# Tail exponentials stacked in rows for two of four head groups, and the heads' scores issued ahead of the previous group's values

## The chip, the cores and the metric

The kernel runs on one core of one Trainium2 chip. The metric is the device time of one execution in microseconds (us), the median over runs. The profiler's times come from one further execution of the same program.

## The reference: what is computed

The input x has 4 sequences of 2048 tokens with 512 channels; the context has 4 sequences of 154 tokens. All is float32. Cut to what matters:

```python
# gated cross attention: 16 heads of 32 channels, 154 keys per head
Q = (layernorm(x) @ Wq.T); K = ctx @ Wk.T; V = ctx @ Wv.T
attn = softmax(Q K^T / sqrt(32)) V                   # per head
x = x + tanh(g_xattn) * (attn @ Wo.T)
# gated feed-forward with a shift by one token
n = layernorm(x); prev = n shifted by one token
xr = mu_r*n + (1-mu_r)*prev; xk = mu_k*n + (1-mu_k)*prev
x = x + tanh(g_ffn) * sigmoid(xr @ W_r.T) * (relu(xk @ W_k.T)**2 @ W_v.T)
```

## The kernel before

The tokens are cut into 16 blocks of 512 (`N`). Block `i` does its attention while TensorE also does the feed-forward of block `i - 1`; block 0 has the projections of the context in that place. Blocks 1 to 14 are one hardware loop, blocks 0 and 15 are written out. `ffn` is true for every block but the first, `pre` for every block but the last. "Later blocks" are blocks 1 to 15.

Every product is made in parts: a number is split into a high part and the rest, and three products are summed (high by high, high by low, low by high; `PRODUCTS`). The order on each engine is written out by hand, and semaphores carry the dependences; each engine runs its own list in order.

The 16 heads are four groups (`g`) of four. For one group the work is:

- `head_scores` (L1512 to L1525, TensorE): scores of the first 128 keys of each of the four heads, one bank `s_bank[j]` for each, as matmuls on a quarter of the array's rows. It waits until all low parts (`p_lo`) of the group before have been made.
- `tail_scores` (L1527 to L1532): the other 26 keys of all four heads in one bank, with 32 rows for each head. It waits until the low part of unit 0 of this group is made, because it writes the same bank.
- `exps` (L791 to L798, ScalarE): for each of the five banks (`n` = 0 to 4, the tails are 4), one exponential into the high part in `pq` (16 bit) and one, in place in the bank, in full precision.
- `p_low` (L1097 to L1099, VectorE): the full exponential minus the high part, into the low part in `pq`.
- `values` (L1534 to L1553, TensorE): the values product into `o_bank` (12 matmuls for the heads, 12 for the tails), and the sums of the exponentials into `d_bank` (8 and 8). They use a quarter of the array's columns each, so that four run beside each other.
- `attend` (L1101 to L1116, VectorE): two transposes, a reciprocal and a product, which make the group's normalised result `attn32`. `attn_high` (ScalarE) and `attn_low` (GpSimd) split it.

Between these, TensorE has products of 12 matmuls of 512 columns of the feed-forward (`ffn_r`, `ffn_v`). In a later block the order on TensorE from group 1 on is: `values(0)`, `head_scores(1)`, `ffn_r(1)`, `tail_scores(1)`, `ffn_v(0)`, `values(1)`, `head_scores(2)`, `ffn_v(1)`, `tail_scores(2)`, `ffn_r(2)`, `values(2)`, `head_scores(3)`, `ffn_r(3)`, `tail_scores(3)`, `ffn_v(2)`, `values(3)`.

During the same groups the next block's input is prepared. VectorE takes its statistics (`moments1`, L1037 to L1042), ScalarE normalises (`norm1_turn`, L742), VectorE turns it (`turn`, L1077: the first two tiles in group 2 before `p_low(2, 2)`, the others after `gated`), and SyncE stores the two halves to memory and loads them again transposed (`store_turned` L346, `load_turned` L353). ScalarE and GpSimd split what was loaded (`xT_high_half` L690, `xT_low_half` L544), VectorE has one part of that (`xT_low_part` L1082) and then does `attend(3)`. After `values(3)` TensorE makes the next block's queries in halves (`query_half`, L1502) and, inside the last of them, the first row maxima (`maxima(i + 1, 0)`, L1478). `maxima(i + 1, 0)` waits for `q_high(i + 1, 0)`, which on ScalarE stands behind `attn_high(i, 3)`.

`gated` (L1126) is VectorE's last step on a feed-forward product. `load_values` (L373, L374) brings the next block's values to SBUF.

Of the kernel before, what the change touches and what calls it, by code (L numbers as in the profile page):

```python
# [17 lines left out]
def flamingo_block(nc, x, ctx_columns, g_xattn, g_ffn, Wq, Wk, Wv, Wo, W_r, W_k, W_v, mu_r, mu_k, out):  # L18
# [34 lines left out]
    with ExitStack() as ctx:  # L53
# [14 lines left out]
        def parts(name):  # L68
# [3 lines left out]
            parts(n) for n in ("WqT", "WoT", "WrT", "WkT2", "WvT2"))  # L72
        xnT_loaded, xnT = parts("xnT")
# [13 lines left out]
        v_tail = sb("v_tail", [P, 2, G, 4, TAIL], F16)  # L87
        ones_main = sb("ones_main", [P, DH], F16)
        ones_tail = sb("ones_tail", [P, 4, DH], F16)
        xa = sb("xa", [P, TT, D], F32)  # L90
        x1 = sb("x1", [P, TT, D], F32)
        pq = sb("pq", [P, 5, 2, N], F16)
        place = sb("place", [P, 8, N], F32)
        mm = sb("mm", [P, TT, P], F32)
# [19 lines left out]
        recip = sb("recip", [P, N // 32], F32)  # L114

# [62 lines left out]
        p_hi, p_full, p_lo = sem("p_hi"), sem("p_full"), sem("p_lo")  # L178
# [49 lines left out]
        K_LOADS, V_LOADS, FIRST_TAILS = 7, 5, 5  # L228
# [62 lines left out]
        def _(sp):  # L291
# [76 lines left out]
            def load_values(i):  # L368
                later(sp, av_done, i * G)
                b = i // PER_BATCH  # L370
                for j in range(4):
                    rows = slice(DH * j, DH * j + DH)
                    sp.dma_start(v_tail[rows, :, :, j, :], vt_scratch[b].rearrange("r s (g j d) -> r s g j d", g=G, j=4)[:, :, :, j, :]).then_inc(v_loaded, 16)  # L373
                sp.dma_start(v_main[:, :, :], v_scratch[b]).then_inc(v_loaded, 16)  # L374
# [94 lines left out]
        def _(pool):  # L469
            done = [0]  # L470

            def link(ins):
# [15 lines left out]

            link(nc.gpsimd.memset(ones_main[:, :], 1.0))
# [4 lines left out]
                                         base=DH - 1, pattern=[[DH, 4], [0, DH]], channel_multiplier=-1))  # L494
            link(nc.gpsimd.memset(tail_rows[:, :], 1.0))
# [9 lines left out]
            link(nc.gpsimd.memset(mm[:, :, :], 0.0))  # L505
# [182 lines left out]
        def _(act):  # L688
# [21 lines left out]
            def kv_high(u):  # L710
                item, kind, n = KV[u]
                act.wait_ge(kv_done, u + 1)
                if item == 1 and kind == "k" and n >= 2:
                    act.wait_ge(later_stored[n - 2], 48)
                elif (item, kind, n) == (1, "v", 0):
                    act.wait_ge(v_stored, 32)
                    act.wait_ge(v_loaded, 16 * V_LOADS)
# [73 lines left out]
            def exps(i, g, n):  # L791
# [72 lines left out]
            def step(i, ffn, pre):  # L864
# [9 lines left out]
                exps(i, 0, 0)  # L874
                exps(i, 0, 1)
# [3 lines left out]
                exps(i, 0, 2)  # L879
                exps(i, 0, 3)  # L880
                if not ffn:
                    kv_high(FIRST_LATER)
                exps(i, 0, 4)
# [6 lines left out]
                for g in range(1, G):  # L890
                    exps(i, g, 0)
                    exps(i, g, 1)
                    attn_high(i, g - 1)
# [4 lines left out]
                    exps(i, g, 2)  # L898
                    exps(i, g, 3)
                    if not ffn and g < 3:  # L900
                        kv_high(FIRST_LATER + 2 * g)
                    exps(i, g, 4)
# [101 lines left out]
        def _(dve):  # L1004
# [80 lines left out]
            def reduce_max(i, r, heads=range(4)):  # L1085

                (g, t), pairs = ROUNDS[r][0], len(ROUNDS[r])
                for j in heads:
                    if r == j == 0:
                        later(dve, mT_done, i)  # L1090
                    dve.wait_ge(max_done, i * MAX_UNITS + 4 * r + j + 1)
                    scores = s_bank[j][:, 0:S * pairs].rearrange("p (n s) -> p n s", n=pairs)
                    column = TAIL * j + g
                    maxima = mm[:, t:t + pairs, column] if ROUNDS[r][-1][1] > t else mm[:, t, column:column + pairs]
                    nc.vector.reduce_max(maxima, scores, AX.X).then_inc(reduced, 1)  # L1095

            def p_low(i, g, n):  # L1097
                dve.wait_ge(p_full, i * SCORE_UNITS + 5 * g + n + 1)
                nc.vector.tensor_tensor(pq[:, n, LO, :], score_bank[5 * g + n][:, :], pq[:, n, HI, :], ALU.subtract).then_inc(p_lo, 1)  # L1099
# [130 lines left out]
            def step(i, ffn, pre):  # L1230
# [16 lines left out]
                p_low(i, 0, 0)  # L1247
                if ffn:
                    xr_low(i - 1, 3)
                p_low(i, 0, 1)  # L1250
                p_low(i, 0, 2)
                p_low(i, 0, 3)
                if not ffn:
                    kv_low_part(FIRST_LATER)
                p_low(i, 0, 4)
# [7 lines left out]
                for g in range(1, G):  # L1263
                    attend(i, g - 1)
                    p_low(i, g, 0)
                    p_low(i, g, 1)
# [7 lines left out]
                    p_low(i, g, 2)  # L1274
                    p_low(i, g, 3)
                    if not ffn and g < 3:
                        kv_low_part(FIRST_LATER + 2 * g)
                    p_low(i, g, 4)
# [130 lines left out]
        def _(pe):  # L1409
# [97 lines left out]
            def maxima_transposed(i):  # L1507
                pe.wait_ge(reduced, (i + 1) * MAX_UNITS)
                later(pe, x2_ready, i * TT - 1)
                transposed(mT_bank, [mm[:, t, :] for t in range(TT)]).then_inc(mT_done, 1)  # L1510
# [23 lines left out]
            def values(i, g, by_pe):  # L1534
                pe.wait_ge(p_lo, i * SCORE_UNITS + 5 * g + 5)
                later(pe, attn32_ready, i * G + g)
                if g == 0:
                    pe.wait_ge(v_loaded, 16 * V_LOADS * (i + 1))
# [3 lines left out]
                for n in range(2):  # L1542
                    for k, (s, q) in enumerate(PRODUCTS):
                        for j in range(4):
                            v = v_main[:, s, DH * (4 * g + j):DH * (4 * g + j + 1)] if n == 0 else v_tail[:, s, g, j, :]
                            nc.tensor.matmul(o_bank[rows(j), :], v, pq[:, 4 if n else j, q, :],  # L1546
                                             start=(n, k) == (0, 0), stop=(n, k) == (1, 2))
                for n in range(2):
                    for q in (HI, LO):
                        for j in range(4):  # L1550
                            one = ones_main[:, :] if n == 0 else ones_tail[:, j, :]
                            ins = nc.tensor.matmul(d_bank[rows(j), :], one, pq[:, 4 if n else j, q, :],  # L1552
                                                   start=(n, q) == (0, HI), stop=(n, q) == (1, LO))  # L1553
# [57 lines left out]
            def ffn_r(i, t):  # L1611
# [3 lines left out]
                else:  # L1615
                    pe.wait_ge(u_ready, i * TT + t)
                product(R_BANK[t][:, :], lambda s, c: buf2[:, s, c, cols(t)], lambda m, c: WrT[:, m, c, :], C,
                        (lambda c: pe.wait_ge(xr_lo, i * C + c + 1)) if t == 0 else None).then_inc(r_done, 1)
# [37 lines left out]
            def step(i, ffn, pre):  # L1656
# [26 lines left out]
                tail_scores(i, 1)  # L1683
                if ffn:
                    ffn_v(i - 1, 0)
                else:
                    keys_or_values(FIRST_LATER + 3)
                values(i, 1, not ffn)

                head_scores(i, 2)  # L1690
                if ffn:
                    ffn_v(i - 1, 1)
                else:
                    keys_or_values(FIRST_LATER + 4)
                tail_scores(i, 2)
                if ffn:
                    ffn_r(i - 1, 2)
                else:
                    keys_or_values(FIRST_LATER + 5)
                values(i, 2, not ffn)  # L1700

                head_scores(i, 3)
                if ffn:
                    ffn_r(i - 1, 3)
                else:
                    keys_or_values(KV_UNITS - 1)
                if not ffn:
                    xT(1, 0)
                tail_scores(i, 3)
                if ffn:  # L1710
                    ffn_v(i - 1, 2)
                else:
# [129 lines left out]
```

## Time and profile before

| | |
|---|---|
| runs | 1353.62 us median of 3 (1349.99 to 1354.55) |
| the profiled execution's own time | 1352.5 us |
| its span | 1350.8 us |
| matmuls on TensorE | 9776, busy 98% of the span |
| VectorE, ScalarE, GpSimd busy | 77%, 58%, 49% |
| mean granted TensorE clock | 0.997 |

The span is the stretch from the first to the last instruction of the profile; the execution's own time has 1.7 us more around it. Busy shares are means over the whole program. In the rows further below, a line of the timeline is a run of equal instructions merged into one: its start and length in us, the engine, the line of the kernel, the operation, what it writes and reads, how many there are, and in brackets how long the engine stood idle before it and which instruction ended that. Matmuls overlap, so that the start of the next line says more than the length of one. PEld is TensorE's weight load, SPq is SyncE's DMA queue.

### The profile page before, as it was taken

How to read it: one execution, taken by the hardware profiler on the slowest of the kernel's cores; microseconds unless marked ns; L12 is line 12 of the kernel's file. 1: busy time of each engine (PE TensorE's matmuls, PEld its weight loads, DVE VectorE, ACT ScalarE, POOL GpSimd, SP SyncE). 2: the span in 40 equal slices, each digit the busy share in tenths (PEclk: the TensorE clock that was granted, in tenths of full speed). 3: DMA queues.
4: the chain of work that ended last, by engine and by line, in shares of the span. 5: the costliest groups of instructions: out<-in, count | busy, mean ns of one | idle time of the engine just before them, and what ended most of it. 6: DMA issues, size and time to landing. Idle time of an engine off the chain costs nothing.

```text
span 1350.8 us, 28900 instructions
## 1 busy us (share of the span) xinstructions
PE 1324.2 (98%) x9776; PEld 992.8 (73%) x9776; DVE 1046.6 (77%) x1983; ACT 778.0 (58%) x1457; POOL 659.6 (49%) x843
## 2 busy tenths in 40 slices
PE   6999999999999999999999999999999999999998
PEld 5667687777768677776877768777776877768777
DVE  6878778787886878778787887878788687877763
ACT  7655737466474655737466473745737465573633
POOL 7524445454444545445454445545445554444434
PEclk9998999999999999999999999999999999999999
DMA  9521312424123242312424222242413324231011
GB/s 311 155 59 48 91 51 78 116 55 128 44 84 77 62 132 54 99 45 77 112 54 132 59 77 66 62 132 54 122 33 85 93 54 139 54 92 48 32 48 40
DMA packets 160732, 113.27 MB, mean 84 GB/s; under 512 B 107456, under 2 KB 122304, under 8 KB 160704
## 3 DMA queue, kind: packets, MB, share of 16 engines
q1 hardware_dynamic: 160704, 112.91, 29.3%
q8 instruction: 16, 0.26, 0.1%
q14 instruction: 12, 0.10, 0.0%
HBM read 72.43 MB, written 35.39 MB: 80 GB/s over the span
## 4 chain that ended last, share of the span: by engine, by line
PE 88%; DVE 8%; ACT 3%; issue 1%; DMA 0%; DVEq 0%; ACTq 0%
PE g_bank L1415 41%; PE g_bank L1606 10%; PE o_bank L1546 7%; PE g_bank L1502 6%; PE s_bank L1520 4%; PE d_bank L1552 4%; PE s_bank L1530 3%; PE s_bank L1415 3%; PE s_bank L1478 3%; DVE buf L1006 2%; DVE o_bank L1194 2%; PE o_bank L1421 1%; DVE d_bank L1194 1%; PE s_bank L1524 1%; PE d_bank L1421 1%
## 5 line engine op out<-in xcount | busy, mean ns | idle before, releaser
L1099 DVE TENSOR_TENSOR pq<-s_bank,pq 128x512 f16<-128x512 f32 x320 | 220.0, 688 | 73.4 <-ACT s_bank L798 72.1
L1095 DVE TENSOR_REDUCE mm<-s_bank 128x3 f32<-128x462 f32 (+1 forms) x384 | 198.8, 578 | 74.6 <-PE s_bank L1478 74.6
L797 ACT ACTIVATE pq<-s_bank 128x512 f16<-128x512 f32 x320 | 194.3, 607 | 101.2 <-PE s_bank L1524 101.2
L798 ACT ACTIVATE s_bank<-s_bank 128x512 f32<-128x512 f32 x320 | 197.0, 616 | 0.0
L1606 PE MATMUL g_bank<-buf,WkT 128*128 128x512 f32 x720 | 189.7, 409 | 3.4 <-DVE buf L1006 3.3
L1415 PE MATMUL g_bank<-WrT,buf 128*128 128x512 f32 x744 | 183.7, 396 | 0.0
L1415 PE MATMUL g_bank<-WoT,buf 128*128 128x512 f32 (+1 forms) x768 | 175.4, 374 | 0.0
L1415 PE MATMUL g_bank<-WvT,buf 128*128 128x512 f32 x708 | 174.3, 395 | 0.0
L1415 PEld LDWEIGHTS g_bank<-WrT,buf 128*128 128x128 f32 x744 | 137.2, 188 | 39.3 <-issue 10.8
L1606 PEld LDWEIGHTS g_bank<-buf,WkT 128*128 128x128 f32 x720 | 131.4, 191 | 43.9 <-DVE buf L1006 9.6
L1415 PEld LDWEIGHTS g_bank<-WvT,buf 128*128 128x128 f32 x708 | 130.7, 188 | 32.4 <-issue 5.4
L568 POOL TENSOR_TENSOR buf<-place,buf 128x512 fp32r<-128x512 f32 x64 | 82.7, 1293 | 141.6 <-ACT buf L690 141.6
L1415 PEld LDWEIGHTS g_bank<-WoT,buf 128*128 128x128 f32 x768 | 131.2, 188 | 26.0
L690 ACT ACTIVATE buf<-place 128x512 fp32r<-128x512 f32 (+1 forms) x132 | 82.7, 626 | 72.6 <-DVE place L1116 46.4
L556 POOL TENSOR_TENSOR buf<-xa,buf 128x512 fp32r<-128x512 f32 x64 | 82.5, 1289 | 84.5 <-ACT xa L776 46.6
L564 POOL TENSOR_TENSOR buf<-place,buf 128x512 fp32r<-128x512 f32 x60 | 78.1, 1301 | 79.9 <-ACT buf L690 79.9
L1415 PE MATMUL g_bank<-xnT,WqT 128*128 128x512 f32 x420 | 110.9, 401 | 0.0
L576 POOL TENSOR_TENSOR x<-place,x 128x512 f32<-128x512 f32 x45 | 57.9, 1287 | 99.3 <-DVE place L1126 99.3
L757 ACT ACTIVATE xa<-x,nb,rstd 128x512 f32<-128x512 f32 x48 | 39.2, 816 | 112.0 <-POOL nb L525 111.8
L1502 PE MATMUL g_bank<-xnT,WqT 128*128 128x256 f32 x672 | 87.9, 287 | 0.0
L1502 PEld LDWEIGHTS g_bank<-xnT,WqT 128*128 128x128 f32 x672 | 82.1, 191 | 7.1 <-issue 5.9
L1415 PEld LDWEIGHTS g_bank<-xnT,WqT 128*128 128x128 f32 x420 | 74.3, 188 | 14.8 <-issue 0.4
(186 smaller groups left out, 2304.6 us busy)
## 6 DMA issues: line engine op xcount, KB each, us to landing
xa<-in_x SPq DMA_DIRECT2D x64, 256.0 KB, 4.2
x<-in_x SPq DMA_DIRECT2D x64, 256.0 KB, 2.8
xt_scratch<-xa SPq DMA_DIRECT2D x28, 512.0 KB, 3.1
xnT_loaded<-xt_scratch SPq DMA_DIRECT2D x112, 128.0 KB, 3.2
out<-x SPq DMA_DIRECT2D x48, 256.0 KB, 2.3
place<-x SPq DMA_DIRECT2D x16, 256.0 KB, 2.4
out<-place SPq DMA_DIRECT2D x16, 256.0 KB, 2.0
k_all<-k_scratch SPq DMA_DIRECT2D x15, 256.0 KB, 3.3
```

The source lines that it names most:

```text
L556: nc.gpsimd.tensor_tensor(buf4[:, LO, g, :], q32[g], buf4[:, HI, g, :].bitcast(F32), ALU.subtract).then_inc(q_lo, 1)
L564: nc.gpsimd.tensor_tensor(buf1[:, LO, c, :], k2[c % 2], buf1[:, HI, c, :].bitcast(F32), ALU.subtract).then_inc(k2_lo, 1)
L568: nc.gpsimd.tensor_tensor(buf3[:, LO, g, :], attn32, buf3[:, HI, g, :].bitcast(F32), ALU.subtract).then_inc(attn_lo, 1)
L690: nc.scalar.activation(dst, src, ACT.Copy).then_inc(done, 1)
L797: nc.scalar.activation(pq[:, n, HI, :], bank[:, :], ACT.Exp, scale=SCALE).then_inc(p_hi, 1)
L798: nc.scalar.activation(bank[:, :], bank[:, :], ACT.Exp, scale=SCALE).then_inc(p_full, 1)
L1095: nc.vector.reduce_max(maxima, scores, AX.X).then_inc(reduced, 1)
L1099: nc.vector.tensor_tensor(pq[:, n, LO, :], score_bank[5 * g + n][:, :], pq[:, n, HI, :], ALU.subtract).then_inc(p_lo, 1)
L1415: ins = nc.tensor.matmul(dst, stationary(s, c), moving(m, c), start=(c, n) == (0, 0), stop=(c, n) == (chunks - 1, len(PRODUCTS) - 1))
L1502: ins = nc.tensor.matmul(tokens_of(Q_BANK[g][:, :], h), WqT[:, s, c, cols(g)], tokens_of(xnT[:, m, c, :], h), start=(n, c) == (0, 0), stop ...
L1546: nc.tensor.matmul(o_bank[rows(j), :], v, pq[:, 4 if n else j, q, :], start=(n, k) == (0, 0), stop=(n, k) == (1, 2))
L1606: ins = nc.tensor.matmul(K_BANK[c][:, :], WkT2[:, s, e, cols(c)], buf3[:, m, e, :], start=(e, n) == (0, 0), stop=(e, n) == (C - 1, len(PRO ...
```

## The change

In later blocks, groups 1 and 3 (`STACKED`) hold the tails' exponentials otherwise. The high part of the first two heads goes to rows 0 to 63 of one 512-column tile and that of the last two to rows 64 to 127 of a second; the low parts go to the other half of the rows. So the high and the low part of one head lie in one column of the array's input. This takes two high exponentials on 64 rows each in place of one on 128, a wait on their end before the full exponential, and two subtractions on 64 rows in place of one. The values product for the tails then has 8 matmuls in place of 12, the sums 4 in place of 8. The values of the tails are loaded to a second set of rows (four more DMAs in `load_values`), and a second pattern of ones (`ones_both`) is made once at the start on GpSimd.

In all groups of later blocks the order on TensorE changes: `head_scores(g + 1)` stands ahead of `values(g)`, and `tail_scores` stands inside the product that follows, ahead of its third chunk of four. So that this can be, the exponentials of even groups go to buffers of their own, `p_even` (in the room of `xnT`'s high part) and `p_even_tail`, and `exps` waits for the values of the group before the last one. On VectorE `attend(g - 1)` moves behind `p_low(g, 0)`, on ScalarE `attn_high(g - 1)` behind `exps(g, 4)`. The tile `mm` of the maxima shrinks from 512 to 140 columns with the blocks' columns laid between each other.

```diff
             def xT_high_half(i, h, part):
                 act.wait_ge(xT_loaded[h], (i - 1) * 64)
+                act.wait_ge(av_done, i * G - 1)
...
-                later(act, av_done, i * G + g)
-                nc.scalar.activation(pq[:, n, HI, :], bank[:, :], ACT.Exp, scale=SCALE).then_inc(p_hi, 1)
+                later(act, av_done, i * G + g - 1 if ffn else i * G + g)
+                place = p_place(ffn, g, n)
+                if n < 4 or not stacked(ffn, g):
+                    nc.scalar.activation(place[:, HI, :], bank[:, :], ACT.Exp, scale=SCALE).then_inc(p_hi, 1)
+                else:
+                    for tile, rows in enumerate(tail_halves):
+                        nc.scalar.activation(place[rows, tile, :], bank[rows, :], ACT.Exp, scale=SCALE).then_inc(p_tail_hi, 1)
+                    act.wait_ge(p_tail_hi, 2 * ((i - 1) * len(STACKED) + STACKED.index(g) + 1))
                 nc.scalar.activation(bank[:, :], bank[:, :], ACT.Exp, scale=SCALE).then_inc(p_full, 1)
...
+                    for tile, rows in enumerate(tail_halves):
+                        ins = nc.vector.tensor_tensor(place[tail_halves[1 - tile], tile, :], bank[rows, :], place[rows, tile, :], ALU.subtract)
+                    ins.then_inc(p_lo, 1)
...
                 for g in range(1, G):
-                    attend(i, g - 1)
-                    p_low(i, g, 0)
-                    p_low(i, g, 1)
+                    if not ffn:
+                        attend(i, g - 1)
+                    p_low(i, g, 0, ffn)
+                    if ffn:
+                        attend(i, g - 1)
+                    p_low(i, g, 1, ffn)
...
+                if stacked(not by_pe, g):
+                    for s in (HI, LO):
+                        for j in range(4):
+                            nc.tensor.matmul(o_bank[rows(j), :], v_tail[:, s, g, j, :], places[4][:, j // 2, :], start=False, stop=s == LO)
...
+                if stacked(not by_pe, g):
+                    for j in range(4):
+                        ins = nc.tensor.matmul(d_bank[rows(j), :], ones_both[:, j % 2, :], places[4][:, j // 2, :], start=False, stop=True)
...
-                values(i, 0, not ffn)
-
-                head_scores(i, 1)
-                if ffn:
-                    ffn_r(i - 1, 1)
+                if ffn:
+                    head_scores(i, 1)
+                values(i, 0, not ffn)
+                if ffn:
+                    ffn_r(i - 1, 1, at(2, lambda: tail_scores(i, 1)))
+                    ffn_v(i - 1, 0)
```

## Rows read from the trace of the kernel before

**Rows 1.** The page's first part, busy time of each engine over the span.

```profile
PE 1324.2 (98%) x9776; PEld 992.8 (73%) x9776; DVE 1046.6 (77%) x1983; ACT 778.0 (58%) x1457; POOL 659.6 (49%) x843
```

**Rows 2.** Timeline of TensorE in one middle block, values(0) to the next block's queries.

```profile
619.01 0.83 PE L1546 MATMUL o_bank<-pq,v_main 128*32 128x512 f16 x12
619.67 0.82 PE L1546 MATMUL o_bank<-pq,v_tail 128*32 128x512 f16 x12
620.31 0.61 PE L1552 MATMUL d_bank<-pq,ones_main 128*32 128x512 f16 x8
620.75 0.61 PE L1552 MATMUL d_bank<-pq,ones_tail 128*32 128x512 f16 x8
621.28 0.74 PE L1520 MATMUL s_bank<-buf,k_all 32*128 32x512 f32 x8
622.41 3.02 PE L1415 MATMUL g_bank<-WrT,buf 128*128 128x512 f32 x12
625.26 0.86 PE L1530 MATMUL s_bank<-buf,k_tail 128*128 128x512 f32 x3
626.19 2.90 PE L1415 MATMUL g_bank<-WvT,buf 128*128 128x512 f32 x12
629.02 0.83 PE L1546 MATMUL o_bank<-pq,v_main 128*32 128x512 f16 x12
651.33 5.53 PE L1502 MATMUL g_bank<-xnT,WqT 128*128 128x256 f32 x44
656.81 0.57 PE L1478 MATMUL s_bank<-k_all,buf 32*128 32x154 f32 x12
```

**Rows 3.** Timeline of ScalarE in the same block: groups 0 and 1.

```profile
620.94 0.63 ACT L690 ACTIVATE buf<-place 128x512 fp32r<-128x512 f32 x1 [1.22 <-POOL place L560]
622.59 0.60 ACT L797 ACTIVATE pq<-s_bank 128x512 f16<-128x512 f32 x1 [1.02 <-PE s_bank L1524]
623.09 0.59 ACT L798 ACTIVATE s_bank<-s_bank 128x512 f32<-128x512 f32 x1
```

**Rows 4.** Timeline of VectorE in the same block: groups 1 and 2.

```profile
628.23 0.69 DVE L1099 TENSOR_TENSOR pq<-s_bank,pq 128x512 f16<-128x512 f32 x1 [0.31 <-ACT s_bank L798]
629.21 0.69 DVE L1126 SCALAR_TENSOR_TENSOR place<-place,g_bank 128x512 f32<-128x512 f32 x1 [0.28 <-PE g_bank L1415]
631.67 0.68 DVE L1110 STREAM_TRANSPOSE place<-d_bank 128x512 f32<-128x512 f32 x1
634.03 1.38 DVE L1099 TENSOR_TENSOR pq<-s_bank,pq 128x512 f16<-128x512 f32 x2
635.32 1.30 DVE L1077 STREAM_TRANSPOSE xa<-place 128x512 f32<-128x512 f32 x2
```

**Rows 5.** Timeline of SyncE's queue in the same block and just ahead of it.

```profile
606.57 0.37 SPq L378 DMA_DIRECT2D out<-place  x1
636.65 0.33 SPq L346 DMA_DIRECT2D xt_scratch<-xa  x1
645.94 2.61 SPq L353 DMA_DIRECT2D xnT_loaded<-xt_scratch  x4
658.71 2.86 SPq L373 DMA_DIRECT2D v_tail<-vt_scratch  x4
```

**Rows 6.** Timeline of ScalarE and VectorE in the same block, behind the second load.

```profile
651.86 1.15 ACT L690 ACTIVATE xnT<-xnT_loaded 128x512 fp32r<-128x512 f32 x2 [2.10 <-DMA xnT_loaded<-xt_scratch]
652.52 0.69 DVE L1082 TENSOR_TENSOR xnT<-xnT_loaded,xnT 128x512 fp32r<-128x512 f32 x1 [2.60 <-ACT xnT L690]
655.64 0.63 ACT L690 ACTIVATE buf<-place 128x512 fp32r<-128x512 f32 x1 [2.62 <-DVE place L1116]
656.17 0.58 ACT L690 ACTIVATE buf<-g_bank 128x512 fp32r<-128x512 f32 x1
```

**Rows 7.** Timeline, the same place six blocks later.

```profile
1134.37 5.53 PE L1502 MATMUL g_bank<-xnT,WqT 128*128 128x256 f32 x44
1137.85 0.63 ACT L690 ACTIVATE buf<-place 128x512 fp32r<-128x512 f32 x1 [2.66 <-DVE place L1116]
1139.83 0.57 PE L1478 MATMUL s_bank<-k_all,buf 32*128 32x154 f32 x12
```

More of the change, by code:

```diff
@@ L72, in flamingo_block @@
             parts(n) for n in ("WqT", "WoT", "WrT", "WkT2", "WvT2"))
+        with nc.sbuf_tensor("p_even", [P, 4, 2, N], F16) as p_even:
+            pass
         xnT_loaded, xnT = parts("xnT")
@@ L114, in flamingo_block, with p_place, stacked @@
         recip = sb("recip", [P, N // 32], F32)
+        def p_place(ffn, g, n):
+            if ffn and g % 2 == 0:
+                return p_even[:, n, :, :] if n < 4 else p_even_tail[:, :, :]
+            return pq[:, n, :, :]
+        tail_halves = (slice(0, 2 * DH), slice(2 * DH, P))
+        STACKED, stacked_groups = (1, 3), slice(1, G, 2)
+        def stacked(ffn, g):
+            return ffn and g in STACKED
         k2 = (place[:, 0, :], place[:, 1, :])
@@ L372, in load_values @@
                     rows = slice(DH * j, DH * j + DH)
-                    sp.dma_start(v_tail[rows, :, :, j, :], vt_scratch[b].rearrange("r s (g j d) -> r s g j d", g=G, j=4)[:, :, :, j, :]).then_inc(v_loaded, 16)
+                    other = slice(DH * ((j + 2) % 4), DH * ((j + 2) % 4) + DH)
+                    tails = vt_scratch[b].rearrange("r s (g j d) -> r s g j d", g=G, j=4)
+                    sp.dma_start(v_tail[rows, :, :, j, :], tails[:, :, :, j, :]).then_inc(v_loaded, 16)
+                    sp.dma_start(v_tail[other, HI, stacked_groups, j, :], tails[:, HI, stacked_groups, j, :]).then_inc(v_loaded, 16)
                 sp.dma_start(v_main[:, :, :], v_scratch[b]).then_inc(v_loaded, 16)
@@ L873, in step @@
                     xr_high(i - 1, 2)
-                exps(i, 0, 0)
-                exps(i, 0, 1)
+                exps(i, 0, 0, ffn)
+                exps(i, 0, 1, ffn)
                 if ffn:
@@ L890, in step @@
                 for g in range(1, G):
-                    exps(i, g, 0)
-                    exps(i, g, 1)
-                    attn_high(i, g - 1)
+                    exps(i, g, 0, ffn)
+                    exps(i, g, 1, ffn)
+                    if not ffn:
+                        attn_high(i, g - 1)
                     if not ffn and g == 3:
@@ L897, in step @@
                         xT_high(i + 1, 0)
-                    exps(i, g, 2)
-                    exps(i, g, 3)
+                    exps(i, g, 2, ffn)
+                    exps(i, g, 3, ffn)
                     if not ffn and g < 3:
                         kv_high(FIRST_LATER + 2 * g)
-                    exps(i, g, 4)
+                    exps(i, g, 4, ffn)
+                    if ffn:
+                        attn_high(i, g - 1)
                     if ffn and pre:
@@ L1092, in reduce_max, with p_low @@
                     scores = s_bank[j][:, 0:S * pairs].rearrange("p (n s) -> p n s", n=pairs)
[L1093 to L1094 removed]
+                    column, stride = TAIL * j + 4 * t + g, 4 if ROUNDS[r][-1][1] > t else 1
+                    maxima = mm[:, column:column + stride * (pairs - 1) + 1:stride]
                     nc.vector.reduce_max(maxima, scores, AX.X).then_inc(reduced, 1)
[L1097 removed]
+            def p_low(i, g, n, ffn):
                 dve.wait_ge(p_full, i * SCORE_UNITS + 5 * g + n + 1)
[L1099 removed]
+                place = p_place(ffn, g, n)
+                bank = score_bank[5 * g + n]
+                if n < 4 or not stacked(ffn, g):
+                    nc.vector.tensor_tensor(place[:, LO, :], bank[:, :], place[:, HI, :], ALU.subtract).then_inc(p_lo, 1)
+                else:
+                    for tile, rows in enumerate(tail_halves):
+                        ins = nc.vector.tensor_tensor(place[tail_halves[1 - tile], tile, :], bank[rows, :], place[rows, tile, :], ALU.subtract)
+                    ins.then_inc(p_lo, 1)
             def attend(i, g):
@@ L1509, in maxima_transposed @@
                 later(pe, x2_ready, i * TT - 1)
-                transposed(mT_bank, [mm[:, t, :] for t in range(TT)]).then_inc(mT_done, 1)
+                transposed(mT_bank, [mm[:, 4 * t:4 * t + P] for t in range(TT)]).then_inc(mT_done, 1)
             def head_scores(i, g):
@@ L1541, in values @@
                     pe.wait_ge(xT_lo, TT + 1)
-                for n in range(2):
+                places = [p_place(not by_pe, g, n) for n in range(5)]
+                for k, (s, q) in enumerate(PRODUCTS):
+                    for j in range(4):
+                        nc.tensor.matmul(o_bank[rows(j), :], v_main[:, s, DH * (4 * g + j):DH * (4 * g + j + 1)], places[j][:, q, :],
+                                         start=k == 0, stop=False)
+                if stacked(not by_pe, g):
+                    for s in (HI, LO):
+                        for j in range(4):
+                            nc.tensor.matmul(o_bank[rows(j), :], v_tail[:, s, g, j, :], places[4][:, j // 2, :], start=False, stop=s == LO)
+                else:
                     for k, (s, q) in enumerate(PRODUCTS):
                         for j in range(4):
[L1545 to L1548, printed above, removed]
+                            nc.tensor.matmul(o_bank[rows(j), :], v_tail[:, s, g, j, :], places[4][:, q, :], start=False, stop=k == 2)
+                for q in (HI, LO):
+                    for j in range(4):
+                        nc.tensor.matmul(d_bank[rows(j), :], ones_main[:, :], places[j][:, q, :], start=q == HI, stop=False)
+                if stacked(not by_pe, g):
+                    for j in range(4):
+                        ins = nc.tensor.matmul(d_bank[rows(j), :], ones_both[:, j % 2, :], places[4][:, j // 2, :], start=False, stop=True)
+                else:
                     for q in (HI, LO):
                         for j in range(4):
-                            one = ones_main[:, :] if n == 0 else ones_tail[:, j, :]
-                            ins = nc.tensor.matmul(d_bank[rows(j), :], one, pq[:, 4 if n else j, q, :],
-                                                   start=(n, q) == (0, HI), stop=(n, q) == (1, LO))
+                            ins = nc.tensor.matmul(d_bank[rows(j), :], ones_tail[:, j, :], places[4][:, q, :], start=False, stop=q == LO)
                 ins.then_inc(av_done, 1)
```

83 lines of the change are left out of this document (47 added, 36 removed).

## Prediction, made before the changed kernel ran

> **What bounds the kernel now.** First the busy line [rows 1]: TensorE is busy for 98% of the span, no other engine for more than 77%. So work taken off TensorE can be worth its time, but only where nothing else stands just behind it. The timelines tell that, and I read them for one middle block, TensorE first. With T for the start of values(1) at 629.02, its queries start at 651.33 (call this point Q, T + 22.31) and the maxima at 656.81 (call it M, Q + 5.48) [rows 2]. Then I looked, on the other engines, for what ends just before TensorE needs it. There are two such places. One is the last low part of each group: the subtraction of group 1 starts at 628.23 and lasts 0.69, so it ends at 628.92, 0.1 ahead of T [rows 2, 4]. The other is M. The chain to it starts with the first pair of turns on VectorE (635.32), goes over store and load (SyncE issues the store at 636.65 and the second load at 645.94), the split on ScalarE at 651.86, VectorE's part at 652.52, then attend(3), attn_high(3) at 655.64, and q_high at 656.17 + 0.58 = 656.75 [rows 4 to 6]. TensorE starts the maxima at 656.81, 0.06 later. So in this block M has no slack at all, although TensorE shows no idle time there.
>
> **What TensorE loses.** The tails' part of a values product is 12 matmuls in 620.31 - 619.67 = 0.64, three rounds of four, so 0.213 a round; the sums over the heads are 8 in 620.75 - 620.31 = 0.44, or 0.22 a round [rows 2]. A stacked group saves one round of each, 0.433. Two groups in 15 blocks: 0.87 a block, 13.0 us in all. This is the whole gross gain.
>
> **Order on TensorE.** Nothing else is removed. values(0) takes 621.28 - 619.01 = 2.27, head_scores 622.41 - 621.28 = 1.13, a product 2.83 to 2.85, tail_scores 626.19 - 625.26 = 0.93 [rows 2], before and after. The trace never shows values behind head_scores. The nearest row is values followed by head_scores, where the last two rounds take 0.53 instead of 0.44 [rows 2]: a boundary is worth about 0.1. With three boundaries a group in either order I take no difference; the bounds are 0.1 less or more in each of 45 places, 4.5 us to either side, of which two thirds lie behind T, where they are partly absorbed (below).
>
> The Trainium skill says on the page "TensorEngine Tiling (Array Packing)", section "Key Properties", that a change of tiling mode drains the array. By that rule the new order, with as many changes, costs what the old one did; if values behind head_scores needed no drain, the sum would be up to 4.5 us better. No row here has that pair.
>
> **ScalarE and VectorE in a stacked group.** Exponentials follow each other every 0.50 (622.59 to 623.09) [rows 3], low parts every 0.65 or less (two in 634.03 to 635.32) [rows 4]. The trace has no exponential on 64 rows. Its cost lies between half a pitch, 0.25, and a full 0.60; I take the full pitch, since the length of the operation in columns stays 512. One more exponential is 0.5, and the wait for its end adds what lies between pitch and length, 0.1, plus a signal, 0.05. The second subtraction is one more pitch, 0.61 (between 0.3 and 1.3, twice the first bound to twice a pitch of 0.65, since it writes other rows than it reads).
>
> The page "ScalarE: Activation LUTs" of the Trainium skill, section "Rules for kernel authors", budgets about 0.3 us for an activation plus 0.83 ns an element; for 512 columns, an estimate from that page, 0.73. No row has it that high (0.60 is the longest in rows 3). By it the chain of group 1 would end 0.2 later, still within its slack.
>
> Where does this fall? *Group 1*, with H1 = 619.01 as the new start of head_scores(1). k2_high(3) holds ScalarE from 620.94, so the exponentials start at 621.45 rather than 1.31 behind H1. Eight take 4.03, the two halves start at 625.48 and 625.97, the full one at 626.62 and ends at 627.24. VectorE: low part 0 at 622.6, attend(0) 623.2 to 625.56 (2.36, from 631.67 to 634.03 [rows 4]), three low parts to 627.39, two halves to 628.7. The next head_scores is due at 629.02. Slack 0.3: no stall. tail_scores(1) is due at H1 + 1.13 + 2.27 + 1.42 = 623.83 and its low part 0 is there at 623.2. *Group 2* (not stacked), counted from T, now the start of head_scores(2): VectorE has gated at T + 0.19, statistics to T + 2.65 (631.67) [rows 4], low part 0 to 3.26, attend(1) to 5.62 (the values end at 1.13 + 1.84 = 2.97, so it does not wait), low part 1 to 6.23, turns to 7.45, three low parts to 9.4. Due at 1.13 + 1.84 + 6.59 = 9.56. Slack 0.15. *Group 3*: its exponentials aren't held up, the end comes about 9.0 behind head_scores(3) and is due at 10.0.
>
> **The point where the gain is lost.** All 0.87 of a block are saved between T and Q: in values(1) and values(3). But the turns end at T + 7.45 before and after (two transposes, 635.32 + 1.22 [rows 4]), because VectorE has the same list of work ahead of them and starts it with gated, at T + 0.19. From there on the chain is DMA: the issue of the first store T + 7.6, the second load issued 645.94, landed 651.86 = T + 22.84 [rows 5, 6]. TensorE gets to Q at T + 21.44 and would start the maxima at T + 26.92; q_high lets it go at T + 27.79, as before. So in this block the whole 0.87 becomes a wait at M.
>
> How much in other blocks? The chain to M is 1.17 long from attn_high(3) (655.64 to 656.81) [rows 2, 6]. Slack at M = (Q + 5.47) - (attn_high(3) + 1.17): 0 in this block; in the one of rows 7, 1139.84 - 1139.02 = 0.82. The 14 blocks 1 to 14, read in the same way, have 0.65, 0.04, 0.14, 0.30, 0.18, 0.82, 0, 0.68, 0.73, 0.76, 0.37, 0.19, 0.82, 0.32; these two rows are the ends. What 0.87 exceeds them by sums to 6.2 us. The last block has no queries behind it and keeps its 0.87.
>
> **Other parts, at no cost.** Four more DMAs in load_values: the four there take SyncE 2.86 [rows 5], so it is free 2.9 later, near 665. A block is (1139.83 - 656.81) / 6 = 80.5 long [rows 2, 7], so the last output's store of 606.57 [rows 5] comes again at 687, 22 later, and the values are needed in the next block. If that cover were gone, keep_x1 would be 2.9 later. attn_high behind exps(g, 4): attend(g) needs attn_low(g - 1), which then ends some 9.3 behind head_scores at the latest, attend(g) comes at about 13. The split of the first half of the next input gets this attn_high ahead of it, but the second product now starts earlier than tail_scores did; I count nothing. The wait on av_done there is for values(2), long done. The small patterns of ones are made on GpSimd in the first 10 us, where it waits for VectorE's statistics: nothing. The maxima's smaller tile: the same number of elements, nothing.
>
> **Sum.** 13.0 - 6.2 = 6.8 us gained. 1352.5 - 6.8 = 1345.7 for an execution like the profiled one. The median of the three runs is 1.1 above it, so **1346.8 us**. Each 0.1 by which the chain to M is longer or shorter in all 14 blocks is worth up to 1.4.
>
> **Rivals.**
> 1. *The chain to M yields.* If the landing of the second load moves with the lighter VectorE (or the turns come 0.4 or more earlier), all 13.0 are kept: 1340.6. For it: the slack at M varies by 0.82 from block to block, so it isn't fixed by T alone. Against it: VectorE has no idle slot between gated and the turns. Values behind head_scores at a cheaper boundary gives a point in between.
> 2. *The chain takes it all.* If the turns come 0.45 later than I count (attend(1) waits for values(1), for which I have only 0.2), hardly any block keeps its gain: 1352.8. For it: the order on VectorE now hangs on values that start 1.13 later than before.
> 3. *The stacked tail becomes the bound of group 1.* Here nothing absorbs it, as it lies ahead of T. Slack 0.3; a lateness beyond it counts 15 times. From 0.75 on the kernel is slower. With subtractions to other rows at the upper bound (2.6 for two instead of 1.3) it is 1.0 too late, 15.0 lost: 1346.8 + 15.0 = 1361.8. For it: ScalarE starts 1.1 later than it could, behind k2_high(3). Against: no row shows an operation whose length depends on rows.
> 4. *The rounds don't get shorter.* If the stacked matmuls don't run four at a time, nothing is saved: 1353.6. Against: their shape is that of the others.
>
> **Chances.** Forecast 0.50, rival 1 0.21, rival 2 0.17, rival 3 0.08, rival 4 0.04. A measurement of this kernel can tell 0.3%, 4.1 us, from no change. The forecast's own range is 1343.5 to 1350; it lies below 1349.5 nearly always. Faster: 0.46 of the forecast, rival 1 whole, 0.02 of rival 2: 0.69. Slower: rival 3 and a little of 2 and 4: 0.09. Same: 0.22. The range for 8 in 10 takes in rival 1 and rival 2: 1340 to 1353.5.
>
> **What would show it.** 9536 matmuls in place of 9776. In the rows of values(1), 8 and 4 matmuls for the tails and 0.43 less time. TensorE idle ahead of L1478 on a release by ScalarE, 0 to 0.87 a block, some 6 in all. The second load landing at T + 22 to 23. VectorE's turns at T + 6.2. I am wrong if the idle time ahead of the maxima isn't there, or if head_scores(2) waits for the low part of the tails.

## The result, and the profile after

| | before | changed |
|---|---|---|
| median of 5 runs each | 1351.86 us (1349.99 to 1354.55) | 1343.04 us (1340.68 to 1343.68) |
| the profiled execution's own time | 1352.5 us | 1340.7 us |
| its span | 1350.8 us | 1339.0 us |

The ratio is 0.9927, 95% interval 0.9915 to 0.994: 8 to 11 us faster, 8.8 between the medians. The forecast was 6.8 us and 1346.8, with a range of 1340 to 1353.5: the time lies in the range, the forecast gain 2.0 below the measured one and outside its interval.

The two profiled executions differ by more, 11.8 us. Some 2.5 of that has nothing to do with the change. In the profile before, 24 matmuls of block 1 took 8.60 us, in the one after 6.06:

```profile
115.95 8.60 PE L1606 MATMUL g_bank<-buf,WkT 128*128 128x512 f32 x24 [1.25 <-DVE buf L1006]
```

```profile
115.33 6.06 PE L1672 MATMUL g_bank<-buf,WkT 128*128 128x512 f32 x24 [1.26 <-DVE buf L1049]
```

The granted clock of the two traces, over the first part of these matmuls (window, its length, busy time of five engines, granted clock as a share of 2.4 GHz, DMA share and GB/s):

```profile
115.90:120.00 4.10, 4.05 (x10) 3.19 (x11) 3.82 (x7) 1.44 (x3) 1.34 (x2) 0.50 0.02 4
```

```profile
115.30:118.00 2.70, 2.67 (x12) 2.17 (x12) 2.43 (x4) 1.21 (x3) 0.38 (x2) 1.00 0.00 0
```

So before, these matmuls began at the lower level, 1.2 GHz. The clock fell in the wait ahead of them (0.69 in the mean from 114.70 to 115.95, 1.00 ahead of that), and that wait is no longer than in the other profile (1.25 against 1.26 us, in brackets), where it stayed at 2.4 GHz. So what follows compares blocks of the loop, where both traces have the clock at 1.00, and not whole spans. From the first queries of the loop to the last, 13 blocks later, it is 1214.87 - 168.29 = 1046.58 us before and 1203.15 - 164.34 = 1038.81 after: 7.8 us less.

The busy line of the page after (as [rows 1]) has 240 matmuls fewer, ScalarE 26.7 us more and VectorE 7.8 us more.

```profile
PE 1309.5 (98%) x9536; PEld 984.1 (73%) x9536; DVE 1054.4 (79%) x2013; ACT 804.7 (60%) x1487; POOL 662.0 (49%) x847
```

The timeline of TensorE in a middle block after, from head_scores(2) on (as [rows 2]; T is now 622.55, Q 644.01, M 649.71):

```profile
622.55 0.74 PE L1574 MATMUL s_bank<-buf,k_all 32*128 32x512 f32 x8
623.69 0.83 PE L1599 MATMUL o_bank<-pq,v_main 128*32 128x512 f16 x12
624.35 0.60 PE L1605 MATMUL o_bank<-pq,v_tail 128*32 128x512 f16 x8
624.78 0.61 PE L1612 MATMUL d_bank<-pq,ones_main 128*32 128x512 f16 x8
625.21 0.39 PE L1615 MATMUL d_bank<-pq,ones_both 128*32 128x512 f16 x4
625.53 1.67 PE L1469 MATMUL g_bank<-WvT,buf 128*128 128x512 f32 x6
...
644.01 5.54 PE L1556 MATMUL g_bank<-xnT,WqT 128*128 128x256 f32 x44
649.71 0.57 PE L1532 MATMUL s_bank<-k_all,buf 32*128 32x154 f32 x12 [0.15 <-ACT buf L722]
```

The values product takes 625.53 - 623.69 = 1.84 in place of 2.27: the 0.43 of the sum. Values behind head_scores come 1.14 behind its start, as the product did before (1.13): the pair that no row had shown costs nearly the same. From T to Q it is 21.46 in place of 22.31. And the last line has what [rows 2] did not have: TensorE waits for ScalarE ahead of the maxima. The chain of waits of the same block, in order of time, says where it comes from (start, length, what):

```profile
628.83 1.22 DVE xa L1120 x2
630.07 2.60 DMA xt_scratch<-xa
...
635.38 3.73 DMA xt_scratch<-xa
...
641.08 3.65 DMA xnT_loaded<-xt_scratch
644.76 0.64 ACT xnT L722
...
646.03 0.72 DVE place L1161
...
649.07 0.59 ACT buf L722
649.71 0.57 PE s_bank L1532 x12
```

From the first turns on VectorE (L1120) it goes over the store, the loads, the split on ScalarE (L722), `attend(3)` (L1161) and `q_high`; until the maxima there is no TensorE on it. Over the whole program the page gives TensorE 69% of the chain, where it had 88% before, and DMA 7%, where it had none.

How long TensorE waits there is best read as M - Q. It is 5.47 without a wait. In the 14 blocks of the profile after it is 5.51, 5.79, 5.67, 5.46, 5.92, 6.01, 5.70, 5.66, 5.54, 5.79, 5.47, 5.58, 5.85, 6.22: 3.6 us of waits in all. TensorE's own list of waits names 4.0 us in 9 places for this line, where it named 1.5 in 2 before, of which 1.3 is in block 0 in both; waits under 0.1 or so are not in it, so the starts are the better measure.

### The profile page after: what moved, and what is told of

It is laid out like the page before. It is cut to its first block, busy times and chain, and to the rows that moved or that the text cites. A ratio compares the mean times of both kernels' runs of the same rounds, so it can differ in the third digit from the quotient of the medians.

```text
span 1339.0 us, 28782 instructions
## 1 busy us (share of the span) xinstructions
PE 1309.5 (98%) x9536; PEld 984.1 (73%) x9536; DVE 1054.4 (79%) x2013; ACT 804.7 (60%) x1487; POOL 662.0 (49%) x847
## 4 chain that ended last, share of the span: by engine, by line
PE 69%; DVE 13%; DMA 7%; ACT 4%; SPq 3%; issue 3%; DVEq 0%; ACTq 0%
PE g_bank L1469 34%; PE g_bank L1672 10%; DMA xt_scratch<-xa 4%; PE s_bank L1574 3%; SPq L374 3%; PE g_bank L1556 3%; PE s_bank L1532 3%; DMA xnT_loaded<-xt_scratch 2%; PE s_bank L1469 2%; PE s_bank L1584 2%; PE o_bank L1599 2%; DVE buf L1049 2%; DVE o_bank L1245 2%; PE o_bank L1475 2%; DVE d_bank L1245 1%
## 5 line engine op out<-in xcount | busy, mean ns | idle before, releaser
L1469 PE MATMUL g_bank<-WrT,buf 128*128 128x512 f32 x744 | 188.6, 396 | 0.0
L1672 PEld LDWEIGHTS g_bank<-buf,WkT 128*128 128x128 f32 x720 | 129.2, 188 | 43.9 <-DVE buf L1049 10.1
L1146 DVE TENSOR_TENSOR pq<-s_bank,pq 128x512 f16<-128x512 f32 x140 | 90.9, 685 | 46.1 <-ACT s_bank L838 46.0
L722 ACT ACTIVATE buf<-place 128x512 fp32r<-128x512 f32 (+1 forms) x132 | 82.6, 626 | 73.5 <-DVE place L1167 46.4
L833 ACT ACTIVATE pq<-s_bank 128x512 f16<-128x512 f32 x140 | 83.4, 596 | 17.2 <-PE s_bank L1578 17.2
L1146 DVE TENSOR_TENSOR p_even<-s_bank,p_even 128x512 f16<-128x512 f32 x120 | 80.0, 677 | 6.1 <-ACT s_bank L838 6.1
```

Of the source, the lines that this page charges most:

```text
L722: nc.scalar.activation(dst, src, ACT.Copy).then_inc(done, 1)
L833: nc.scalar.activation(place[:, HI, :], bank[:, :], ACT.Exp, scale=SCALE).then_inc(p_hi, 1)
L1146: nc.vector.tensor_tensor(place[:, LO, :], bank[:, :], place[:, HI, :], ALU.subtract).then_inc(p_lo, 1)
L1469: ins = nc.tensor.matmul(dst, stationary(s, c), moving(m, c), start=(c, n) == (0, 0), stop=(c, n) == (chunks - 1, len(PRODUCTS) - 1))
L1672: ins = nc.tensor.matmul(K_BANK[c][:, :], WkT2[:, s, e, cols(c)], buf3[:, m, e, :], start=(e, n) == (0, 0), stop=(e, n) == (C - 1, len(PRO ...
```

## Experiments

The runs came in three groups, each on a chip of its own. Each group had its own runs of the kernel before, with medians of 1352.57 (the first four below), 1353.74 and 1352.90; a ratio is to those. Across groups only ratios compare well, and the profiles show what the times can't tell.

**The order alone.** `STACKED` is empty; the further loads still put values into rows that the unstacked products read, so the tails' sums are others, with the same number and shape of instructions.

```diff
-        STACKED, stacked_groups = (1, 3), slice(1, G, 2)
+        STACKED, stacked_groups = (), slice(1, G, 2)
```

> The changed kernel with no group stacked (STACKED empty); the new order, the second set of buffers and the four further loads stay. Theory (the gain is TensorE's removed rounds, 13.0 us, less a new wait ahead of the first maxima of 14 blocks): nothing is removed, Q is again 22.3 behind T, the maxima start 5.47 behind Q in every block without a wait, and the time is that of before, 1351.9 (within 1.5). Rival (the order itself gives part of the 8.8 us, since it takes TensorE's waits for low parts away): 2 to 5 us faster than before.

Measured: 1353.15, ratio 1.0002 (0.9992 to 1.0012). The new order by itself is worth nothing; the gain is the removed rounds. The trace shows a small cost of the order: an unstacked group takes TensorE 10.04 in place of 10.01, and blocks without a wait are 80.56 apart in place of 80.50, some 0.9 us in all, less than the times can tell. One thing in its trace was not as the theory had it. M - Q was up to 5.84, 1.2 us of waits in all: values(1) are longer here than in the changed kernel (2.27), and attend(1) waits for them, so that the turns start at T + 6.52 (T = 626.78) and not at T + 6.20:

```profile
630.31 0.72 DVE L1161 STREAM_TRANSPOSE place<-d_bank 128x512 f32<-128x512 f32 x1 [0.23 <-PE d_bank L1619]
...
633.30 1.29 DVE L1120 STREAM_TRANSPOSE xa<-place 128x512 f32<-128x512 f32 x2
```

That is the mechanism of the prediction's second rival. It is at work here: the turns start 0.3 later against T than in the changed kernel, where values(1) are 0.43 shorter and attend(1) doesn't wait.

**Stacking in the old order.**

```diff
-                if ffn:
-                    head_scores(i, 1)
                 values(i, 0, not ffn)
-                if not ffn:
-                    head_scores(i, 1)
-                if ffn:
-                    ffn_r(i - 1, 1, at(2, lambda: tail_scores(i, 1)))
+                head_scores(i, 1)
+                if ffn:
+                    ffn_r(i - 1, 1)
...
+                tail_scores(i, 1)
```

> Groups 1 and 3 stacked, but the order of before on TensorE (values ahead of the next group's head scores, tail scores between two products), attend ahead of the first low part, attn_high behind the second exponential. Theory: in the old order the low part of the tails ended 0.1 ahead of values(1) and values(3); one more exponential with its wait (0.65) and one more subtraction (0.65) put it 1.2 to 1.3 later, so TensorE waits about 1.15 in 30 places. Net per block 2 x 1.15 - 0.87 = 1.4 us slower, 21 in all: 1373. Rival (ScalarE and VectorE have room in the old order too, the new order is not needed): 1343 or better.

Measured: 1378.61, ratio 1.0191 (1.0175 to 1.0208). TensorE's waits, in its own list:

```profile
PE o_bank L1593 <- DVE pq L1146: 36.4, 30, 1.2
```

Thirty waits of 1.21. By the starts each costs 1.29: values(1) come 640.92 - 636.80 = 4.12 behind the product ahead of them, in place of 2.83. So a block should be 2 x 1.29 - 0.87 = 1.7 longer; the blocks are 82.23 apart in place of 80.50, and 15 of them make the 26.0 measured. The 21 expected had each wait 0.14 too short. The two edits belong together: stacking alone loses 26 us, the order alone gains nothing, both gain 7 to 9. The new order is worth something only as room for the longer tails of a stacked group.

**The turns 0.6 earlier, and 0.6 later.** Nothing but the place of two instructions on VectorE, to see whether the wait ahead of the maxima hangs on them.

```diff
+                    if ffn and pre and g == 2:
+                        turn(i + 1, 0)
+                        turn(i + 1, 1)
                     p_low(i, g, 1, ffn)
-                    if ffn and pre and g == 2:
-                        turn(i + 1, 0)
-                        turn(i + 1, 1)
                     p_low(i, g, 2, ffn)
```

> The changed kernel with VectorE's first two turns ahead of the second low part of group 2 instead of behind it, nothing else. Theory (the wait ahead of the first maxima, 3.6 us in the profile, hangs on the turns through store, load, split and attend(3)): the chain starts 0.6 earlier, the wait shrinks to 0.15 in one block, the time falls by 3.4 to 1339.6. Rival (the wait hangs on the load's landing for reasons of its own, such as the queue's other transfers, or another resource takes its place): no change, 1343.

> The changed kernel with the same two turns behind the third low part of group 2, 0.6 later. Theory: every one of the 14 blocks waits, 0.86 in the mean, 12.0 us in place of 3.6: 8.4 slower than the changed kernel, 1351.4, so that nearly the whole gain over the kernel before is gone. Rival (the landing isn't set by the turns): 1343.

Measured: 1340.64, ratio 0.9912 (0.9896 to 0.9928), and 1350.74, ratio 0.9985 (0.9972 to 0.9999). Earlier turns leave 0.6 us of waits, all in the block where the load landed late (M - Q = 6.10). Later turns make it a wait in 13 of the 14 blocks: M - Q is 5.47 in one and 5.81 to 6.97 in the others, 11.2 us of waits in all, where 12.0 were expected. TensorE's own list, which puts the same waits too low, has

```profile
PE s_bank L1532 <- ACT buf L722: 8.3, 14, 1.3
```

1.2 us of placement of two transposes moves the kernel by 10.1 us, from 1340.6 to 1350.7, and the waits by 10.6. That the wait ahead of the maxima hangs on the turns is shown. Against the changed kernel, which has runs in other groups only, the times give 2.4 us less (3.4 expected) and 7.7 more (8.4 expected). The first isn't clear of noise by the times alone: the changed kernel's ratios are 0.9927 and, again below, 0.9956. For it the waits in the traces stand, 3.6 and 5.7 in the changed kernel and 0.6 here.

**The changed kernel again, and a third group stacked in it.**

> The changed kernel once more, beside the next three on one chip. Theory: 1343.0 (within 1.5), that is 8 to 10 us below before.

```diff
-        STACKED, stacked_groups = (1, 3), slice(1, G, 2)
+        STACKED, stacked_groups = (1, 2, 3), slice(1, G)
```

> The changed kernel with group 2 stacked as well (STACKED = 1, 2, 3, and the loads for three groups), nothing moved. TensorE has 0.43 less in 15 blocks, 6.5 us. Theory: nothing of it comes through. In group 2 VectorE ends its low parts 0.33 ahead of the next head scores and now needs 0.65 more, so TensorE waits about 0.4 there, and the chain to the first maxima is fixed by the turns anyway: 1342.6 (within 1.5). Rival (the time follows TensorE's work): 1336.5.

Measured: the changed kernel 1346.45 (1342.93 to 1350.32), ratio 0.9956 (0.9941 to 0.9971), and three groups 1346.24, ratio 0.9946 (0.9929 to 0.9964). The changed kernel is 7.3 below before here and was 8.8 below. Its profile had M - Q at 5.88 in the mean and up to 6.47, 5.7 us of waits in place of 3.6; the time from the turns to the split of the second load was 16.20 in the mean, 16.04 in the first profile, with the same turns at Q - 15.27. So the size of the wait moves with when the loads land, between blocks (15.8 to 16.8) and between executions. From the first queries of the loop to the last this profile has 1041.62, 5.0 less than before. The profiled execution was the fastest of its group, 1342.93; what waits the others had isn't known. The kernel before, which has no such wait in its profile, spreads by 6 us over its own runs (1349.72 to 1355.66 in this group), so most of the spread of single runs has other causes.

The third group gives nothing, as expected. TensorE has 120 matmuls less and waits for the low part of group 2:

```profile
PE s_bank L1574 <- DVE p_even_tail L1149: 6.6, 14, 0.5
```

6.5 us of rounds are removed, 6.6 us of waits are new, and the waits ahead of the maxima stay (5.5 by the starts).

**Two moves on VectorE, with two and with three groups.** The statistics of the third tile go into 1.41 us of idle ahead of group 1's first low part, the first turns go ahead of group 2's first low part.

```diff
                     moments1(i + 1, 0, ffn)
                     moments1(i + 1, 1, ffn)
+                    if ffn:
+                        moments1(i + 1, 2, ffn)
                 for g in range(1, G):
+                    if ffn and pre and g == 2:
+                        turn(i + 1, 0)
+                        turn(i + 1, 1)
...
-                        moments1(i + 1, 2, ffn)
+                        if not ffn:
+                            moments1(i + 1, 2, ffn)
                         moments1(i + 1, 3, ffn)
```

> The changed kernel with two groups stacked and two moves on VectorE: the statistics of the third tile go from behind group 1 into the 1.4 us idle ahead of group 1's first low part, and the first two turns go ahead of group 2's first low part. The turns start at about T + 1.7 instead of T + 6.2. Theory: the wait ahead of the first maxima is gone in all blocks, also where the load lands late (1.15 behind Q at worst): 1339.2, 3.8 below the changed kernel. Rival (something else waits next, such as the second pair of turns or the key loads): 1341 or more.

> Both moves and group 2 stacked as well. Theory: VectorE's work in group 2 now ends 0.5 ahead of the next head scores in spite of the second subtraction, and the chain to the maxima has over 3 us to spare, so TensorE's 6.5 us come through whole: 1332.7, 10.3 below the changed kernel. Rival (VectorE is the bound of group 2): about 1336.

Measured: two groups 1339.77, ratio 0.9905 (0.9886 to 0.9925); three groups 1333.65, ratio 0.9855 (0.9836 to 0.9875), and once more on another chip (the same file) 1335.22, ratio 0.9869 (0.9853 to 0.9885).

> Groups 1, 2 and 3 stacked with both moves, once more on this chip: 1333.6 (within 1.5), about 19 us below before.

This is the fastest kernel of the study, 18 to 20 us below before and 12.8 below the changed one beside it. With two groups the moves are worth 6.7 us by the medians and 5.1 by the traces (1036.53 from the first queries of the loop to the last, against 1041.62); with three, another 6.1. In the profile of its first run VectorE's list of group 2, with head_scores(3) due at 630.71:

```profile
622.83 1.27 DVE L1120 STREAM_TRANSPOSE xa<-place 128x512 f32<-128x512 f32 x2
...
628.88 1.39 DVE L1149 TENSOR_TENSOR p_even_tail<-s_bank,p_even_tail 64x512 f16<-64x512 f32 x2
```

The turns start at T + 1.73 (T = 621.10), and the low parts end at 630.27, 0.44 ahead. With two groups ScalarE does the four splits of both loads in one run from Q - 2.97, so that the second load is split at Q - 1.93 in all 14 blocks: a time without spread, as no landing in this study has. So the DMAs no longer set it.

**The fourth group.** Also with both moves.

```diff
-        STACKED, stacked_groups = (1, 3), slice(1, G, 2)
+        STACKED, stacked_groups = (0, 1, 2, 3), slice(0, G)
```

> All four groups stacked, with both moves on VectorE. TensorE has another 6.5 us less. Theory: group 0 has no product between its tail scores and the end to give room (ffn_r(0) alone), and its low part ended 0.2 to 0.3 ahead of head_scores(1); with 1.3 more on ScalarE and VectorE TensorE waits 1.05 there in 15 blocks, so this is 9 us slower than with three groups: 1343. Rival (the time follows TensorE's work): 1327.

Measured: 1349.2, ratio 0.9976 (0.9965 to 0.9988), 14 us slower than three groups, more than the 9 expected.

```profile
PE s_bank L1577 <- DVE p_even_tail L1149: 17.7, 15, 1.2
```

The wait at head_scores(1) is 1.19 where 1.05 was expected, and head_scores(2) comes 3.02 behind the start of ffn_v(0) (625.35 to 628.37) instead of 2.82. So group 1 is late as well, by 0.2: values(0) are 0.43 shorter, and the low parts of group 1 end only 0.19 sooner behind head_scores(1) (9.67, with three groups 9.86). By this sum four groups cost 17.7 + 3.0 - 6.5 = 14.2 us.

**The kernel before, with one move.** Is the chain to the maxima a cost there too? Same diff for the statistics, in the kernel before.

> The kernel before with one move: the statistics of the third tile stand ahead of attend(0) instead of behind group 1, so that the first turns start 0.9 earlier against values(1). Theory (before, the chain to the first maxima ended 0 to 0.8 ahead of TensorE and cost next to nothing; it became a cost only through the change): 0 to 1 us faster than before. Rival (the chain was already a cost of the kernel before, and earlier turns alone give the 3 us that they give in the changed kernel): 3 us faster.

Measured: 1353.31, ratio 1.0005 (0.9994 to 1.0015). But the run doesn't test the question, because the turns didn't move. They start at T + 6.30 and Q - 16.01, as before. attend(1) could start only 0.26 earlier, since it now waits for values(1), and the second low part of group 2, ahead of the turns, then waits for ScalarE. In a block with T = 550.75 (these start at T + 5.69 and T + 6.30):

```profile
556.44 0.69 DVE L1099 TENSOR_TENSOR pq<-s_bank,pq 128x512 f16<-128x512 f32 x1 [0.23 <-ACT s_bank L798]
557.05 1.29 DVE L1077 STREAM_TRANSPOSE xa<-place 128x512 f32<-128x512 f32 x2
```

The answer comes from the profile before: M - Q is 5.46 to 5.48 in all 14 blocks, so the chain cost it nothing there. In this run's own profile one block of 14 has 5.68, where the load landed late.

## Why the prediction was right

The mechanism was the one forecast: what the rounds save on TensorE comes back in part as a wait ahead of the maxima, on a chain that starts with the turns. The forecast gain of 6.8 was too small because the term for that wait, 6.2 us, was too large.

**What TensorE loses: right, a little less comes through.** 0.87 a block was the term. With the chain out of the way the profile of the earlier turns has blocks 79.68 apart (queries from 246.43 to 1043.23, ten blocks), the profile before 80.50: 0.82 arrives, 12.3 us in 15 blocks. The other 0.05 is the order: against the 80.56 of the order alone it is 0.88. Four matmuls in columns still take 0.22 a round (8 in 624.78 - 624.35 = 0.43).

**Order on TensorE: right within its bounds.** It was taken at nothing, with bounds of 4.5 us. The time of the order alone shows nothing (ratio 1.0002), the traces 0.06 a block.

**A stacked group on ScalarE and VectorE: right, a little short.** Instructions on 64 rows took as long as those on 128: 592 ns for the exponential, 689 ns for the subtraction that writes to other rows, against 0.60 and 0.69 in [rows 3, 4]. The split cost ScalarE 0.76 rather than 0.65: the halves start at 618.96, the full exponential at 620.20, where it would have started at 619.44. The low parts of group 1 ended at 622.37, 0.18 ahead of T, where 0.3 was counted; those of group 2 ended 0.33 ahead of head_scores(3), where 0.15 was counted.

```profile
618.96 1.21 ACT L836 ACTIVATE pq<-s_bank 64x512 f16<-64x512 f32 x2
620.20 0.58 ACT L838 ACTIVATE s_bank<-s_bank 128x512 f32<-128x512 f32 x1
```

```profile
620.98 1.39 DVE L1149 TENSOR_TENSOR pq<-s_bank,pq 64x512 f16<-64x512 f32 x2
```

The Trainium skill's budget for an activation (page "ScalarE: Activation LUTs", section "Rules for kernel authors": about 0.3 us plus 0.83 ns an element, by estimate 0.73 for 512) is above the 0.592 measured. That row is for an activation with its bias as a pointer operand; the exponentials here pass a scale and no bias (L833), so it was not the row for them, and the measurement decides. The budget has no term for rows, which agrees with 592 ns on 64 rows and 596 on 128 (means of L836 and of L833 into `pq`).

**The point where the gain is lost: the place right, the size too large.** The chain is the one named, step by step, and TensorE waits where it was said to. The term was 6.2 us; measured were 3.6 and 5.7 in two profiles. Two things made it smaller.

The first was in the prediction's own rows. It let the turns end at T + 7.45 before and after. Before, they end at 635.32 + 1.22 = 636.54, T + 7.52, and start at T + 6.30; after, they start at T + 6.20, because the low part in front of them no longer waits for ScalarE. So Q moved towards the turns by 16.01 - 15.27 = 0.74, not by 0.87. With 0.74 against the same 14 leads the sum is 4.5.

The second is that the time from the turns to the split, which the leads carry, was taken from one profile. It is drawn anew in each execution: in the mean 16.10 before, 16.04 in the first profile after and 16.20 in the second. 0.06 less in 14 blocks makes 4.5 into some 3.7, 0.10 more into some 5.9, by estimate; 3.6 and 5.7 were measured.

These terms add up. 13 blocks at 0.82, less the waits that fall between the first queries of the loop and the last (2.85 and 5.70), are 7.8 and 5.0 us; the two profiles are 7.8 and 5.0 shorter there than before. For the whole program it is, by estimate, 12.3 - 3.6 = 8.7 and 12.3 - 5.7 = 6.6. The medians gave 8.8 and 7.3. How near these come is partly luck, as a median is not the profiled execution: the second profile's took 1342.93, 3.5 below the median of its group.

**Other parts: right.** The four further loads, attn_high and the maxima's tile show nothing; the order alone (first experiment) has them all and stands at 1.0002.

**The rivals.** The first (all 13 kept) did not happen in the change itself; the two moves on VectorE get nearly there. The second's mechanism was seen in the order alone. The third, the tails of group 1 as the bound, missed by 0.18; in group 0 it is what makes the fourth group a loss. The fourth is out: the stacked values product is 0.43 shorter.

## What to carry to other kernels

When the busiest engine is at 98%, read for each point where it could wait how long before it the awaited work ended. A gain on that engine is worth only the smallest such lead between the place of the saving and the place of the wait; here 0.87 saved met leads of 0 to 0.82 on a chain of transposes, two stores and two loads. Then start that chain earlier by moving short work into an idle slot far ahead of it: here two moves gave 5 to 7 us for no added work, and room for a third group. And look in the trace whether the move moved the chain: the same move of the statistics in the kernel before left the turns where they were.

A saving that lengthens another engine's work needs room made first. Stacked tails lost 26 us in the old order and gained 7 to 9 in the new one.

## What was not expected of the hardware

The granted clock fell ahead of the same stretch of block 1 in some executions of the same program and not in others. The two profiles of the fastest kernel, one file, have its 24 matmuls in 6.05 us at a granted clock of 1.00 and in 7.24 us, begun at 0.50, both behind a wait of 1.26. In the two profiles compared above it was 8.60 and 6.06, behind 1.25 and 1.26. So it makes 1.2 us of difference between two executions of one program, and 2.5 between those two profiles. The landing of the same loads in the same place of a block varied by 0.9 us (15.64 to 16.54 from the turns to the split) within one execution of the kernel before, and by 1.5 (15.53 to 17.01) with the turns 0.6 earlier.
